# Routed experts of a decoder layer: the stores of the pairs' results are begun by ScalarE, two pairs behind, instead of by SyncE

## The reference, cut to what matters

```python
tidx, tw = _route(x, router_weight, e_bias)      # 4 of 16 experts for each token
g = jnp.einsum('th,eih->tei', x, gate_w); u = jnp.einsum('th,eih->tei', x, up_w)
h = jax.nn.silu(g) * u                           # inner width 128
yo = jnp.einsum('tei,ehi->teh', h, down_w)
routed = jnp.einsum('te,teh->th', combine, yo)   # combine holds the 4 weights of a token
out = layernorm(x + routed + shared(x))          # two shared experts for all tokens
```

## Time and profile before

| | us |
|---|---|
| median of 3 runs | 2109.72 (2103.54 to 2112.45) |
| profiled execution | 2096.8 |
| its span | 2095.1 |
| PE busy | 1615.6 (77%) |
| DVE busy | 1336.0 (64%) |
| ACT busy | 890.6 (43%) |
| POOL busy | 650.2 (31%) |
| mean granted TensorE clock | 0.88 of full speed |

### The profile page before, as it was taken

The page is one execution under the profiler, slowest core; times in us unless marked ns, Lnnn a source line. Parts: engine busy times, 40 slices in busy tenths (PEclk is TensorE's granted clock), DMA queues, the critical chain, the costliest instruction groups (busy, mean ns, idle before and its releaser), DMA issues. The chain is left out here.

```text
span 2095.1 us, 37385 instructions
## 1 busy us (share of the span) xinstructions
PE 1615.6 (77%) x11882; PEld 974.9 (47%) x11882; DVE 1336.0 (64%) x3773; ACT 890.6 (43%) x1430; POOL 650.2 (31%) x857
## 2 busy tenths in 40 slices
PE   7979999997887799899899999574335376776760
PEld 4646676775553233333333333152334276766660
DVE  7954554554898788788788887065867133444553
ACT  5534554553332166566566666511121033333330
POOL 2143333311332411111111111262676502034444
PEclk9989999998998599999999999787677688888885
DMA  5698676561587643533433443776364334446563
GB/s 168 224 186 141 112 118 106 104 157 63 173 253 189 85 62 52 94 60 52 86 61 60 78 125 154 277 231 219 108 206 143 125 116 142 126 146 179 180 192 108
DMA packets 207511, 285.91 MB, mean 136 GB/s; under 512 B 55122, under 2 KB 162322, under 8 KB 200430
## 3 DMA queue, kind: packets, MB, share of 16 engines
q1 hardware_dynamic: 168830, 202.39, 36.1%
q0 software_dynamic: 22560, 66.62, 14.9%
q10 hardware_dynamic: 15952, 14.63, 2.8%
HBM read 154.24 MB, written 128.92 MB: 135 GB/s over the span
## 5 line engine op out<-in xcount | busy, mean ns | idle before, releaser
L1471 ACT ACTIVATE sa_prob<-sa_ps_s 128x1024 f32<-128x1024 f32 (+3 forms) x480 | 376.3, 825 | 280.6 <-PE sa_ps_s L1380 199.9
L1530 DVE CUSTOM_DVE_ANT_0 sa_ps_m<-sa_ps_m,sf_later 128x282 f32<-128x282 f32 (+4 forms) x640 | 278.4, 460 | 53.4 <-PE sa_ps_m L1353 52.0
L1533 DVE TENSOR_REDUCE sa_piece_max<-sa_ps_m 128x1 f32<-128x512 f32 x384 | 259.1, 687 | 43.5 <-PE sa_ps_m L1353 42.9
L1507 POOL TENSOR_SCALAR_AFFINE_SELECT sa_prob<-sa_prob 128x256 f32<-128x256 f32 x256 | 102.2, 406 | 499.3 <-ACT sa_prob L1471 496.7
L1353 PE MATMUL sa_ps_m<-sa_k,sa_q 96*128 96x512 bf16 (+4 forms) x768 | 210.3, 334 | 21.0 <-DVE sa_max_parts L1561 7.4
L1353 PEld LDWEIGHTS sa_ps_m<-sa_k,sa_q 96*128 96x128 bf16 x768 | 66.4, 99 | 241.7 <-issue 110.7
L2206 POOL DMA_INDIRECT mo_picked<-s_ys,mp_row x128 | 124.3, 971 | 173.8 <-DMA s_ys<-mo_y 135.0
L1380 PE MATMUL sa_ps_s<-sa_q,sa_k 99*128 99x512 bf16 (+3 forms) x672 | 160.8, 334 | 2.1 <-ACT sa_prob L1471 2.0
L735 DVE TENSOR_TENSOR la_att<-la_ps_att,lf_cap 128x512 f32<-128x512 f32 x128 | 88.3, 690 | 108.3 <-PE la_ps_att L643 108.3
L643 PE MATMUL la_ps_att<-la_phi_qT,la_phi_kT 128*128 128x128 f32 x1024 | 147.3, 288 | 12.8 <-issue 11.9
L688 ACT ACTIVATE la_phi_kT<-la_ps_kT 128x512 f32<-128x512 f32 x128 | 76.4, 597 | 188.8 <-PE la_ps_kT L624 188.8
(11 more groups left out here) (300 smaller groups left out, 3645.4 us busy)
## 6 DMA issues: line engine op xcount, KB each, us to landing
s_xs<-sa_zero SPq DMA_DIRECT2D x18, 1024.0 KB, 10.0
mo_rows<-s_xs SPq DMA_DIRECT2D x72, 256.0 KB, 3.2
s_ys<-mo_y SPq DMA_DIRECT2D x72, 256.0 KB, 2.2
la_q<-s_q_parts POOLq DMA_DIRECT2D x72, 128.0 KB, 6.0
la_k<-s_k_parts POOLq DMA_DIRECT2D x72, 128.0 KB, 7.8
sa_q<-s_q_parts SPq DMA_DIRECT2D x72, 128.0 KB, 5.0
sa_k<-s_k_parts SPq DMA_DIRECT2D x66, 128.0 KB, 7.0
s_y<-la_y SPq DMA_DIRECT2D x16, 512.0 KB, 3.8
```

The lines of the kernel that those rows point to most:

```text
L1471: nc.scalar.activation(dst, src, ACT.Exp, scale=HD ** -0.5).then_inc(expd[s], 1)
L1507: nc.gpsimd.affine_select(out=square, in_=square, compare_op=ALU.is_ge, fill=0.0, base=0, pattern=[[0, 2], [1, P]], channel_multiplier=-1) ...
L1530: nc.vector.tensor_tensor_reduce(ps_m[:, s, 0:hi - lo], ps_m[:, s, 0:hi - lo], later[:, BANK + lo - first:BANK + hi - first], 1.0, -BIG, A ...
L1533: nc.vector.tensor_reduce(piece_max[:, j, t, n:n + 1], ps_m[:, s, 0:hi - lo], AX.X, ALU.max).then_inc(piece_done[s], 1)
```

## The change

SyncE no longer stores the results; its program between two row loads loses the wait for `y_done` and the store. ScalarE begins the store of pair q-2 in its step q, between `activate(q+1)` and `round_h(q)`, and the last two stores behind its last `take_y`. The wait for `y_done` goes with the store. Nothing else changes.

```diff
             for q in range(PAIRS):
                 if q + SLOTS < PAIRS:
                     load_rows(q + SLOTS)
-                sp.wait_ge(y_done, q + 1)
-                sp.dma_start(io["ys"][list_rows(q)].rearrange("(s p) c -> p s c", p=P), y[:, q % SLOTS]).then_inc(y_out[q % SLOTS], 16)
                 while closed < NT and combine_at(closed, TOPK - 1) + 5 <= q:
                     store_out(closed)
...
+            def store_y(q):
+                act.wait_ge(y_done, q + 1)
+                act.dma_start(io["ys"][list_rows(q)].rearrange("(s p) c -> p s c", p=P), y[:, q % SLOTS]).then_inc(y_out[q % SLOTS], 16)
+
...
                 if q + 1 < PAIRS:
                     activate(q + 1)
+                if q >= 2:
+                    store_y(q - 2)
                 round_h(q)
                 if q:
                     take_y(q - 1)
             take_y(PAIRS - 1)
+            store_y(PAIRS - 2)
+            store_y(PAIRS - 1)
```

## The result

The changed kernel took 2018.1 us in the median of four runs (2011.6 to 2021.7), against 2109.4 before (2103.5 to 2112.5): a ratio of 0.957, interval 0.953 to 0.960. The prediction was 2015, range 1997 to 2057.

A forecast was written before the change was run, and what follows sets the result against it. Row loads stuck behind SyncE's wait for results bound the early pairs; GpSimd with VectorE set the rest. First gathers at 1733, 1788, 1852 (tiles 0, 1, 3), tile 7 at 1964, plus 35.65: span 2000, median 2015 us, range 1997 to 2057.

The forecast's parts named there:

- only issue time is saved: Rival: earlier loads queue in the DMA engines and land as late as now; 14 us gained, 2095; chance 0.04.
- The step: Time per pair before the gathers: 2.85 us, lower bound 2.78, before 5.07.
- SyncE's stops at `store_out`: SyncE still waits at tile stores; costed at nothing, 14 us without the cover of three more steps.
- The rival of a 4 us step: Offsets' gap and falling clock, or ScalarE's 1.2 us begins, hold the step near 4 us; median 2045, chance 0.18.
- The first two: Legs from first copy to tile 0's first gather, predicted 47.7 us, and from there to tile 1's, 56 us.
- the stop at tile 0's fourth choice: VectorE adds tile 0's fourth gathered choice late, holding TensorE: 7 us, taken as 10 with the clock.
- the leg from tile 1 to tile 3: From tile 1's first gather to tile 3's, needing pair 47: 64 us.
- that from tile 3 to tile 7: Leg between these tiles' first gathers, set by GpSimd's chain: 4 x 27.4 = 110, plus 2 us.
- steps that come late to a combination: Allowance in the leg from tile 3 to tile 7, on top of the chain: 2 us.
- the gathers hold the pairs more: Rival: VectorE's stops for gathers delay the pairs the next tile needs, at half clock; median 2046, chance 0.14.
- 27 to 28 us a tile from tile 3 on: Sign of a right forecast: spacing of tiles from tile 3 on, where GpSimd's chain rules.
- VectorE's waits for gathers: Sign of a right forecast: these waits grow from little to tens of us.

The follow-up runs named there:

- the spread combinations: Changed kernel with a tile's combinations 3, 5, 7, 9 pairs behind its start, not 2, 3, 5, 6, and 10 pairs between tiles, not 6: 2010.2 us.
- The late root: Changed kernel with combinations at 3, 5, 7, 9, 8 pairs between tiles, GpSimd's root behind the next tile's first eight gathers (tiles 1 to 6): 1969.7 us.
- the store at once: Changed kernel with each store right behind its copy on ScalarE instead of in the next step: 2025.9 us.

## Why the prediction was right, and where it was off

*What binds.* The load behind the store in SyncE's order was the cause. Two kernels that leave SyncE the stores, one by order and one by slots, give the same gain; one that gives the stores away but keeps the wait loses 51 of 91 us. This is shown; that the 41 us left there are the earlier load and the clock is in part argued.

*The Trainium skill's rule* ("DMA: Bandwidth & Descriptors", section "Issuing engines are not separate DMA queues") holds as far as it goes: stores on ScalarE or on SyncE, same time. The rival drawn beside it, that only issue time is saved, falls: the gain was six times its 14 us. But the issue time is worth more than that rival reckoned: with the late loads begun 0.4 us earlier, the gain was 23 us on one queue and 41 with the stores on ScalarE, and the turns show that the clock is part of it.

*The step.* Predicted 2.85, measured 2.76: the lower bound. In these 15 steps the offsets' read doesn't show, and the clock stands at 1.00. First gather 4.88 us behind its copy, predicted 4.9. ScalarE's begin 0.37, predicted 0.39. SyncE's stops at `store_out` cost nothing, as said: 108.3 us of waiting, and one row wait of 0.6 us. The rival of a 4 us step falls.

*The legs.* The first two were 1.4 and 2.5 us shorter than predicted; the stop at tile 0's fourth choice, which I had put at 10 us, was 9.4 (copy 15 to copy 31 in 53.6 us, less 16 x 2.76). The two terms that were mis-sized are the leg from tile 1 to tile 3 (64, measured 70.2) and that from tile 3 to tile 7 (112, measured 116.8). For the second I had counted 2 us for steps that come late to a combination. That was wrong in kind: VectorE was there in time, and the gathers landed late. The chain of waits after shows it for tile 2, whose last gather took 6.6 us to land, and for the store of pair 47 (start, us, what):

```profile
1840.03 6.62 DMA mo_picked<-s_ys,mp_row
...
1857.33 4.34 DMA s_ys<-mo_y
```

VectorE stood for the whole of the 4.57 us before that tile's fourth combination:

```profile
1846.74 1.67 DVE L2247 SCALAR_TENSOR_TENSOR mo_acc<-mo_picked,mp_weight,mo_acc 128x256 f32<-128x256 f32 x4 [4.57 <-DMA mo_picked<-s_ys,mp_row]
```

So tile 2 took 30.0 us from its first gather to its root (1850.56 - 1820.56), where the chain of 27.4 has some 26. Then pair 47's copy came at 1855.51, right behind the stop, and its store took 4.3 us to land, against 2.2 in the median before, so that tile 3 began 7.0 us behind the copy instead of 4.9. In the second leg, the fourth combination came 5.1, 6.2, 4.9 and 3.0 us behind the begin of the last gather in tiles 3 to 6, and 3.0 in tile 6 of the kernel before. These are 7.2 us more in four tiles, all that the leg has above 4 x 27.4, where I had put 2. I had read the 27.4 us where the pairs were done (last copy at 2043.4, last gather of tile 6 at 2051.4) and used them for tiles beside which pairs still ran; after the change, too, only tile 6 gathers last behind the pairs (last copy at 1962.8, last gather at 1971.3). That the pairs' transfers slow the gathers fits this, but no run shows it by itself. The rival "the gathers hold the pairs more" has the right direction, at a third of its size (11 us in the two legs, against 31 between spans of 2000 and 2031), and in the second leg late gathers, not held pairs, made the difference.

The stage lost 87.5 us in place of 95. That the median still came within 3 us of the forecast is partly luck: the short first legs made up for 3.9 of the 11.0 us, and the medians differ by 91.3 us, not 87.5. Of the signs that I had named, 27 to 28 us a tile from tile 3 on held only for the last of the four (29.1, 30.7, 29.6 and 27.4), and VectorE's waits for gathers grew not from little but from 40.1 to 78.6 us.

*What sets the end.* I wrote that from tile 3 on the chain rules and the pairs hardly matter; the spread combinations show it, with 61 us less for the pairs and 3 less from tile 3 to tile 7. The late root shows that the chain's own 7 us between tiles can go: a leg of 21.9 us in place of 27.4. My expectation of the spread kernel forgot one thing: I let the chain run at 27.4 us from tile 1 on, but a later place for a combination makes it longer.

## What to carry to other kernels

When an engine's program mixes loads that run ahead with stores that follow results, look for a load that stands behind a wait for a result; moving the store back in the same order, or two more slots, cured it here as well as another engine did. Count the new bound before counting the gain: here 71 steps at 2.76 in place of 5.07 us are 164 us, of which 87.5 reached the end, and the next 50 us (a stage of 272.1 us in place of 322.5) lay in where the combinations and one small instruction (the root) stand in their engines' orders. A gap in which the clock falls costs more than its own length: 0.4 us more of idle time went with 1.9 us more for a turn, so a few tenths of a us in each turn can be worth tens in a stage.

## What the runs showed that I had not expected

- The same 48 matmuls took 7.60 us in one turn and 9.52 in the next, at a granted clock of 1.00 and 0.82, in one kernel with one order. The clock stayed at 1.00 in 3 of 23 turns before, and in 7 and 11 of 23 in the two kernels whose late loads begin 0.4 us earlier.
- A read of offsets into TensorE's registers costs nothing visible in the changed kernel before the gathers, and some 0.9 us in every fourth pair of the kernel with the store at once, though it is done in every second pair and ScalarE is as late in those without the gap.
- While the pairs ran, the last gather of a tile took up to 6.6 us to land, and VectorE stood waiting for it; in tile 6, with the pairs done, it was in VectorE's hands 3.0 us behind its begin.
